# Graph layer with pre-norm: means centred by bfloat16 products, masks as ScalarE signs, a two-part edge product

## What is computed

```python
h = maximum(layernorm(x, axis=-1), 0)              # (x - mean) / sqrt(var + 1e-5), then relu
deg = maximum(segment_sum(ones, dst, N), 1); norm = deg ** -0.5
h_src, h_dst = h[src], h[dst]
msg = h_src @ W1 + (h_src * h_dst) @ W2
msg = msg * (norm[src] * norm[dst])
h_N = segment_sum(msg, dst, N) + h @ W1
h = where(h_N >= 0, h_N, 0.2 * h_N)
out = x + h / maximum(l2norm(h, axis=1), 1e-12)
```

## Time and profile before

| | us |
|---|---|
| median of 3 runs | 928.2 (927.44 to 931.21) |
| the profiled execution | 928.79 |
| its span | 927.1 |
| VectorE busy | 870.1 |
| TensorE busy | 734.7 |
| ScalarE busy | 711.0 |
| GpSimd busy | 682.0 |

### The profile page before, as it was taken

How to read it: one execution, slowest core, us unless ns; L and a number is a source line. 1 busy time by engine, 2 the same in 40 slices (tenths; PEclk the granted TensorE clock), 3 DMA queues, 4 the chain that set the end, 5 groups by cost and what they waited for, 6 DMA issues and landing times.

```text
span 927.1 us, 21508 instructions
## 1 busy us (share of the span) xinstructions
PE 734.7 (79%) x6104; PEld 713.7 (77%) x6104; DVE 870.1 (94%) x2878; ACT 711.0 (77%) x2944; POOL 682.0 (74%) x694
## 2 busy tenths in 40 slices
PE   1499888888987988888878898798798887988820
PEld 1398878888887987888877888798788887988810
DVE  6789999999999999999999999999999999999980
ACT  0079887797887987887879788797888888779950
POOL 1777888888788788787788887888888887833472
PEclk9999998898998998998989899898999999889965
DMA  2813746646645655755754664675665665653532
GB/s 71 304 50 90 242 155 196 232 162 201 237 163 197 238 173 188 241 181 180 234 201 164 209 236 165 207 239 165 207 238 168 200 247 166 210 201 131 172 138 60
DMA packets 68804, 172.90 MB, mean 186 GB/s; under 512 B 14383, under 2 KB 34514, under 8 KB 62434
## 3 DMA queue, kind: packets, MB, share of 16 engines
q1 hardware_dynamic: 49868, 135.41, 43.1%
q0 software_dynamic: 18816, 36.08, 12.7%
HBM read 96.89 MB, written 77.04 MB: 188 GB/s over the span
## 4 chain that ended last, share of the span: by engine, by line
DVE 79%; issue 10%; PE 3%; ACT 3%; DMA 1%; DVEq 1%; POOL 0%; SPq 0%; POOLq 0%; ACTq 0%
DVE bst L784 20%; DVE xo L829 19%; DVE ybuf L837 10%; DVE cjk L753 7%; DVE agg L859 5%; DVE oe L821 5%; DVE ye L942 3%; DVE ge L745 2%; DVE ge L746 2%; ACT junk L973 1%; DMA xin<-in_x 1%; PE pt L1106 1%; DVE scs L876 1%; DVE rd L907 1%; DVE d L765 1%
## 5 line engine op out<-in xcount | busy, mean ns | idle before, releaser
L1106 PE MATMUL pt<-nident,bst 128*128 128x128 f32 x1568 | 300.5, 296 | 0.0
L467 POOL DMA_INDIRECT out<-oe,sstage x196 | 234.7, 1198 | 60.3 <-issue 59.1
L1106 PEld LDWEIGHTS pt<-nident,bst 128*128 128x128 f32 x1568 | 265.0, 212 | 0.0
L462 POOL DMA_INDIRECT xs<-in_x,stage x196 | 215.5, 1099 | 53.3 <-issue 52.7
L462 POOL DMA_INDIRECT xd<-in_x,stage x196 | 208.8, 1065 | 59.7 <-issue 59.7
L1116 PE MATMUL pu<-w,ct 128*128 128x128 f32 x1568 | 222.5, 293 | 22.4 <-ACT ct L957 22.4
L1103 PE MATMUL pt<-ident,xin 128*128 128x128 f32 x784 | 230.8, 294 | 7.9 <-DVE bst L784 4.8
L973 ACT ACTIVATE junk<-ybuf 128x128 bf16<-128x128 f32 x784 | 233.3, 306 | 0.7 <-DVE ybuf L837 0.7
L829 DVE SCALAR_TENSOR_TENSOR xo<-ybuf,rd,xin 128x128 f32<-128x128 f32 x784 | 226.6, 341 | 0.0
L1116 PEld LDWEIGHTS pu<-w,ct 128*128 128x128 f32 x1568 | 202.3, 205 | 29.4 <-ACT ct L957 25.8
L957 ACT ACTIVATE ct<-pt 128x512 f32<-128x512 f32 x196 | 116.3, 593 | 55.1 <-PE pt L1106 53.9
(11 more groups left out here) (136 smaller groups left out, 1165.2 us busy)
## 6 DMA issues: line engine op xcount, KB each, us to landing
xin<-in_x SPq DMA_DIRECT2D x96, 512.0 KB, 4.5
out<-xo SPq DMA_DIRECT2D x48, 1024.0 KB
srow<-src_rows SPq DMA_DIRECT2D x49, 256.0 KB, 6.9
edge_rows<-oe SPq DMA_DIRECT2D x49, 256.0 KB
same<-same_segment SPq DMA_DIRECT2D x49, 128.0 KB, 6.2
xs<-in_x,stage POOLq DMA_INDIRECT x196, 2.9
xd<-in_x,stage POOLq DMA_INDIRECT x196, 3.7
out<-oe,sstage POOLq DMA_INDIRECT x196
```

Of the source, the lines that this page charges most:

```text
L462: pool.indirect_dma_start(out=to, out_offset=None, in_=rows, in_offset=bass.IndirectOffsetOnAxis(ap=index, axis=0), bounds_check=limit, oo ...
L467: pool.indirect_dma_start(out=out, out_offset=bass.IndirectOffsetOnAxis(ap=index, axis=0), in_=rows, in_offset=None, bounds_check=row_limi ...
L1106: last = pe.matmul(pt[:, q % 2, f], mean[:, s.buf(0, 2), col:col + 1].to_broadcast([P, D]), nident[:], start=False, stop=True)
```

## The change

There are three edits.

1. *Means.* `bn_stats` leaves the mean as float32. VectorE now splits it into three bfloat16 parts by taking upper halves: `mean_rest(s, d, 0)` writes the mean less its upper half over the count's word, `mean_rest(s, d, 1)` writes that less its own upper half over `m2`'s word (after `stats_guard` has read it). The 48 upper halves of a partition (`parts`) are turned by one bfloat16 product (`turn_means`, into `pe_m`), ScalarE copies the result to `mt` (`copy_means`), and `turn_quarter` adds, instead of the float32 product with `nident`, a bfloat16 product of `pickb` (minus one in the three rows of that column, broadcast) with `mt`.
2. *Masks.* `row_signs` on ScalarE takes the place of `row_masks` on VectorE: sign(srow - first + 0.5) and sign(srow - first - 0.5), with tables and carry halved, so that `lookup` has two one-column products a tile. `fdp` gets one more DMA in the start.
3. *Edge product.* VectorE adds `agg` onto `hdt` after `prod`, and the product with `agg` goes.

The diff, cut to its core:

```diff
+        parts = [bst[:, h, 0:TD * 3].bitcast(BF16)[:, 1::2] for h in range(2)]
+        upper = bst[:, :, 0:TD * 3].rearrange("p b (t w) -> p b w t", w=3)
...
-            dve.tensor_scalar(nident[:], ident[:], -1.0, None, ALU.mult).then_inc(s_const, 1)
+            thirds = ident[0:3 * TD, 0:3 * TD].rearrange("p (t w) -> p t w", w=3)
+            dve.tensor_reduce(pick[:], thirds, AX.X, ALU.add, negate=True).then_inc(s_const, 1)
...
+            dve.tensor_scalar(edge[:, 0:1], first[:], -1.0, 0.5, ALU.mult, ALU.add)
+            dve.tensor_scalar(edge[:, 1:2], first[:], -1.0, -0.5, ALU.mult, ALU.add).then_inc(s_first, 1)
...
-            def row_masks(s, d, i=None):
-                dve.wait_ge(srow_loaded[s.buf(d)], s.dma(d))
-                if i is None or i + d >= 2:
-                    dve.wait_ge(lk_done, s(d - 1) * 2)
-                dve.tensor_scalar(ge[:, h, 0, :], srow[:, s.buf(d), :], first[:, 0:1], None, ALU.is_ge)
-                dve.tensor_scalar(ge[:, h, 1, :], srow[:, s.buf(d), :], first[:, 0:1], None, ALU.is_equal
-                                  ).then_inc(ge_done, 1)
...
+            def mean_rest(s, d, k):
+                b = s.buf(d, 2)
+                dve.wait_ge(bn_done, s(d + 1))
+                if k:
+                    dve.wait_ge(rest_done, s(d + 1))
+                word, to = ((mean[:, b, 0:TD], upper[:, b, 0, :]), (upper[:, b, 0, :], upper[:, b, 2, :]))[k]
+                high = bst[:, b, 0:TD * 3].bitcast(BF16)[:, (3 if k == 0 else 1)::6]
+                dve.tensor_tensor(to, word, high, ALU.subtract).then_inc((rest_done, parts_done)[k], 1)
...
-                    dve.tensor_tensor(prod[:, hh, :], agg[:, hh, :], hdt[:, hh, :], ALU.mult).then_inc(prod_done, 1)
+                    dve.tensor_tensor(prod[:, hh, :], agg[:, hh, :], hdt[:, hh, :], ALU.mult)
+                    dve.tensor_tensor(hdt[:, hh, :], agg[:, hh, :], hdt[:, hh, :], ALU.add).then_inc(prod_done, 1)
...
-                        dve.wait_ge(t_done, s() * NQ)
+                        dve.wait_ge(mt_done, s())
...
+            def row_signs(s, d, i=None):
+                h = s.buf(d, 2)
+                act.wait_ge(srow_loaded[s.buf(d)], s.dma(d))
+                if i is None or i + d >= 2:
+                    act.wait_ge(lk_done, s(d - 1) * 2)
+                for sign in range(2):
+                    last = act.activation(ge[:, h, sign, :], srow[:, s.buf(d), :], ACT.Sign, bias=edge[:, sign:sign + 1])
+                last.then_inc(ge_done, 1)
+            def copy_means(s, d):
+                act.wait_ge(mt_done, s(d + 1))
+                act.copy(mt[:], pe_m[0:3 * TD, 0:P]).then_inc(mt_evac, 1)
...
+            def turn_means(s, d):
+                pe.wait_ge(parts_done, s(d + 1))
+                pe.matmul(pe_m[0:3 * TD, 0:P], parts[s.buf(d, 2)], identb[:], start=True, stop=True).then_inc(mt_done, 1)
...
-                        last = pe.matmul(pt[:, q % 2, f], mean[:, s.buf(0, 2), col:col + 1].to_broadcast([P, D]),
-                                         nident[:], start=False, stop=True)
+                        if q == 0 and t == 0:
+                            pe.wait_ge(mt_evac, s(1))
+                        last = pe.matmul(pt[:, q % 2, f], pickb[:, col:col + 1].to_broadcast([3 * TD, P]), mt[:], start=False, stop=True)
...
-                        pe.matmul(pe_m[:, f], agg[:, h, f], w1[:], start=False, stop=False)
```

More of the change, by code:

```diff
@@ L204, in gnn_preln_kernel @@
         s_const = sem("s_const")
+        s_pick = sem("s_pick")
         s_ch = sem("s_ch")
@@ L267, in gnn_preln_kernel @@
         ye_done = sem("ye_done")
+        rest_done = sem("rest_done")
+        parts_done = sem("parts_done")
+        mt_done = sem("mt_done")
+        mt_evac = sem("mt_evac")
         t_done = sem("t_done")
@@ L844, in _ @@
             stats_guard(Step(0, 0), 0)
+            for k in range(2):
+                mean_rest(Step(0, 0), 0, k)
             def do(s, i):
```

65 lines of the change are left out of this document (46 added, 19 removed).

## The result

The changed kernel takes **945.75 us** (942.25 to 946.95, 4 runs) where the kernel before takes 928.97 (927.44 to 931.21, 4 runs): 1.0168 times as long, interval 1.015 to 1.0186. The forecast was 930.8 us with a range from 926 to 940, and the time lies above both.

The account below looks back on a forecast made before the run. The prediction took VectorE to bound the kernel; steady VectorE work plus 2.3, start plus 1.0 and tail minus 0.7 made plus 2.6 us, against the median 930.8 us, with an 8 in 10 range of 926 to 940.

Parts of the forecast that it names:

- VectorE's sum: VectorE's steps: addition 29.8, subtractions 9.6, masks minus 36.3, hidden subtractions minus 0.8, together plus 2.3 us.
- The masks: VectorE's two mask instructions, removed from 46 steps at 0.79 us each: 36.3 us saved.
- The two subtractions: VectorE's two 128x16 subtractions in 48 steps, 0.10 us each: plus 9.6 us, minus 0.8 for eight possibly hidden.
- signs of being wrong: VectorE waiting for TensorE or ScalarE in steady steps, addition far from 0.62 us, or steps shorter than 17.3 us.
- The rival with dear small instructions: VectorE's subtractions cost 0.19 us each, 8.6 us more in all: 939.4 us; chance 0.14.
- so TensorE has about 3.2 us less a step: TensorE per step: sixteen cheaper centring products save 2.2 to 2.6 us, dropped agg products 0.9, additions cost 0.2.
- Worth nothing in the steady part: TensorE's 3.2 us less a step lies beside VectorE, so it gains no time in steady steps.
- TensorE falls to the low clock: Rival: TensorE mostly at low clock, holding up VectorE from 68% of work; at 75% some 964 us; chance 0.05.
- The 1.6 us of cover: ScalarE's squares of ye keep some 1.6 of 2.7 us lead before VectorE's maximum; cost nothing.
- The start: TensorE turns step 0 2.3 us later, cheaper pairs give back 2.5: plus 1.0 us, bounds minus 0.5 and plus 3.
- The tail: Last edge product starts 0.62 us later but loses four of twelve products at the low clock: minus 0.7 us.
- The unpriced waits with registers: Removed and added VectorE waits in the loop's 24 steps: between minus 4 and plus 4 us, not counted.

Follow-up runs that it names:

- only_masks_3: Kernel before with the masks made as signs by ScalarE and nothing else changed: 905.7 us, 0.9756 times before.
- only_sum: Kernel before with the sum of the edge product on VectorE and nothing else changed: 960.83 us, 1.0331 times before.
- no_means: Changed kernel with the means edit undone (float32 centring products of 128 rows as before), masks as signs and edge sum kept: 923.45 us, 0.9921 times before.
- padded_3: Changed kernel with turned means and picking column filled with zeros from 48 to 128 rows: 931.7 us, 1.0023 times before.
- f32_turned: Changed kernel with the means turned once in float32, unsplit, in 16 rows, without VectorE's two subtractions: 1344.3 us, 1.4424 times before.
- grouped: Changed kernel with each quarter's four transposes first and then its four bfloat16 products: 931.41 us, 1.0017 times before.
- no_sum: Changed kernel with only the edge sum undone, the product with agg back on TensorE: 917.85 us, 0.9881 times before.
- padded_no_sum_2: Changed kernel with centring products zero-filled to 128 rows and the edge product in three parts again, no VectorE addition: 904.9 us, 0.972 times before.
- f32_padded_2: f32_turned with the turned means and picking column filled with zeros from 16 to 128 rows: 926.4 us, 0.9955 times before.

## Why the prediction was wrong, point by point

**VectorE's sum was nearly right, and not in each term.** I forecast 873 us busy, it is 868.4. The addition is one of 0.60 us from start to start (715.65 to 716.25), 0.62 forecast. The masks I put at 0.79 us a step; an undisturbed step gets shorter by 0.73, from before to only_masks_3 (17.33 to 16.60) as from only_sum to no_means (17.95 to 17.22). The two subtractions I put at 0.10 us each, 9.6 in all, less 0.8 for eight that idle time might hide. VectorE's timeline, with the change:

```profile
722.65 0.11 DVE L822 TENSOR_SCALAR guard<-bst 128x16 f32<-128x16 f32 x1
722.67 0.17 DVE L833 TENSOR_TENSOR bst<-bst 128x16 f32<-128x16 f32 x1
722.77 0.61 DVE L839 SCALAR_TENSOR_TENSOR oe<-ye,rd,xd 128x128 f32<-128x128 f32 x2
...
723.64 0.17 DVE L833 TENSOR_TENSOR bst<-bst 128x16 f32<-128x16 f32 x1
723.72 0.61 DVE L839 SCALAR_TENSOR_TENSOR oe<-ye,rd,xd 128x128 f32<-128x128 f32 x2
```

And the same place before the change:

```profile
728.43 0.11 DVE L814 TENSOR_SCALAR guard<-bst 128x16 f32<-128x16 f32 x1
728.55 0.61 DVE L821 SCALAR_TENSOR_TENSOR oe<-ye,rd,xd 128x128 f32<-128x128 f32 x2
```

From the guard to the outputs it takes 0.12 us with the first subtraction in between and 0.12 without it (median of 46 steps, in both traces). So the first is free in every step, not in eight, and the second costs 0.08: 3.8 us in all for the 8.8 of the sum. With this the undisturbed step came out 0.07 us *shorter* than before and not 0.05 longer, which is one of the signs of being wrong that the forecast named; VectorE's waits for ScalarE in steady steps are another. The rival with dear small instructions is out, though its time of 939.4 was nearer to the result than the forecast.

Whole times agree better with the sum than the steps do, and that is luck. In padded_3 the two steps in which the second pass of the hardware loop begins take 41.3 us from scan to scan (436.47 to 477.75) and 37.4 before the change (438.51 to 475.95), with two waits in them that the forecast had no term for:

```profile
457.09 1.28 DVE L881 TENSOR_TENSOR_SCAN agg<-same,agg,pe_s 128x512 f32<-128x512 bf16 x1 [3.25 <-issue]
462.90 0.77 DVE L857 SCALAR_TENSOR_TENSOR ybuf<-ybuf 128x512 f32<-128x512 f32 x1 [2.92 <-ACT ybuf L1007]
```

Over the kernels of the table, f32_turned left out, these two steps take between 35.8 us (only_masks_3) and 41.8 (only_sum), and no edit explains which. So 4.4 of the 8.3 us from no_means to padded_3, and 4.9 of the 37.3 us from only_sum to no_means (960.8 - 923.5), come from there.

**The step that failed is TensorE's**: "a bfloat16 product is one pass [...] so 0.06 to 0.085", "so TensorE has about 3.2 us less a step". I took the price of the product from the lookups, whose neighbours have 128 rows like themselves, and a difference in rows was in no row of the trace and not in my bounds. The product among its like is as quick as that (0.08 in grouped), but a pair costs 0.42 us and not 0.18: over 16 pairs 3.8 us a step more than forecast, 1.4 more than before. That turns "3.2 us less a step" into some 0.6 more at full clock. With full rows the pair is 0.17 and the whole kernel takes 931.7, 0.9 from the forecast, a nearness that owes something to luck, as said.

**"Worth nothing in the steady part" was the second half of it.** I had only asked what a quicker TensorE is worth, and not what a slower one costs. It is late in single steps, and there its clock is low: the rival "TensorE falls to the low clock" had 0.05, and its mechanism is in the trace, but not as I priced it. I asked for 68% of the work at the low level in the mean, and over the span the granted clock fell only from 0.912 to 0.867 in the profiled executions (0.875 to 0.897 in the other three of the changed kernel). Yet it isn't spread. From 100 to 860 us I cut the traces into windows of 1 us. Of these 16% lie below 0.75 before, 25% in the changed kernel, 17% in padded_3; the longest run of such windows is 7 us before, 20 and 21 us in the changed kernel (from 725 and 796 on), 7 in padded_3. A stretch of 20 us is longer than a step, and a step that is late by 2 us stops VectorE, whatever the mean says.

How much of the 14 us is the longer pair and how much the low clock is not settled, but two kernels speak against either of them alone. In no_sum's profiled execution, 913.5 us, the pair is as dear (0.42 us, 737.13 to 737.55), but the granted clock is 0.935, with one run of 14 low windows and none else over 7. From the third scan to the last it takes 773.0 us, padded_no_sum_2 773.2: there the dear pair costs the steady part nothing, and 6.9 of the 7.5 us between the two spans are lost by the third scan. (The slower executions of no_sum, up to 923.08 us, have no trace.) And the ten executions of grouped have a mean granted clock of 0.859 to 0.887, no higher than the changed kernel's 0.867 to 0.897, and take 929.6 to 935.7 us: with a cheaper pair, and low runs of 10 us at most, a low mean clock costs little. So the traces point to the two together, a dear pair in a long low stretch; no run holds the one fixed and moves the other.

**ScalarE.** Busy 776.6 us, 775 forecast. A sign takes 0.62 us from start to start (752.84 to 754.08 for two), I had 0.57. The Trainium skill ("ScalarE: Activation LUTs", What ACT_TABLE_LOAD costs) gives 280 ns and 0.833 ns an element for an activation with a bias from memory, less some 93 ns where two follow each other: 0.61 us, and the trace agrees. The 1.6 us of cover held as long as TensorE was on time: in padded_3, with the same signs, VectorE waits for those squares twice, 3.7 us in all and never between 100 and 860 us (before the change twice, 3.5 us), against 8 times and 8.8 us in the changed kernel. So the lateness of ScalarE there is TensorE's, passed on.

**The start** was put at plus 1.0 with bounds minus 0.5 and plus 3; the first scan comes 3.1 us later, the third 5.2. The step that failed is the same: TensorE begins its pairs at 44.10, before the 44.5 that I worked out, but the low-clock pair was to be 0.33 and is 0.62 there (44.74 to 45.36). With full rows it is 0.32 and the first scan comes at 56.52, 0.2 *earlier* than before.

**The tail** was put at minus 0.7: from the last scan to the end it takes 42.3 us, 42.6 before; the two steps ahead of that scan take 29.1 us where they took 26.5, which the forecast didn't have.

**The unpriced waits with registers** in the loop, 0.2 us a step either way, did nothing that can be seen inside a pass: the loop stretch is full to 173.21 us as before. Where the second pass begins, the two steps spoken of above take 39.8 us in the changed kernel (446.35 to 486.14), 2.4 more than before.

## What to carry to other kernels

A TensorE product that contracts over fewer rows than the products beside it is not cheap for its few rows: it can cost the overlap of weight loads, here 0.25 us for each pair, and zeros in the missing rows (or products of one kind in a row) give it back. When an engine off the critical path gets a new kind of instruction, bound its price upwards too and ask from which lateness in a *single* step it reaches the bounding engine; a mean clock or a mean busy share doesn't answer that. A small instruction next to a wait of its own engine can be free: compare the distance of its neighbours with and without it. And a saving on the bounding engine is worth its full sum only until the next limit: the masks' 36.3 us brought 24 where waits for input transfers came next.

## What the runs showed of the hardware

- Weight loads and rows: a pair of a 128-row float32 transpose and a product, at full clock, from start to start: bfloat16 128 rows 0.17 us, 48 rows 0.42; float32 128 rows 0.33, 16 rows 0.67. At the low clock: bfloat16 128 rows 0.32 (in padded_3, 703.93 to 704.25), 48 rows 0.62. Fewer rows were never quicker here. Between 48 and 128 rows nothing was tried.
- The clock: in the kernel before, padded_3 and no_means, where all these products have 128 rows, stretches at 1.2 GHz last 7 us at most, by 1 us windows, and 4 us in f32_padded_2, whose granted clock is 0.97. With 48 rows between the transposes they reach 20 and 21 us in the changed kernel, 14 in no_sum (there only once) and 10 in grouped, and with 16 rows 21 in f32_turned, where 64% of the windows are low. In those over 10 us of the changed kernel and of f32_turned TensorE is busy in every window from its start to its end. A TensorE that is busy without a gap is thus no sign of a full clock. Why the stretches are longer there no run here tells.
- Small instructions on VectorE: a subtraction on 128x16 values costs 0.08 us from start to start ahead of the edge outputs, and nothing behind the reciprocal and the guard, where the next start comes 0.12 us after the guard with or without it.
